# Thirty-two products of a zeroed tile at the head of the tensor engine's program, in a two-layer graph attention kernel

## What is computed

```
scores = q @ k.T * scaling + adj
ctx    = softmax(scores) @ v
x1     = rmsnorm(x + ctx @ wo + bo)
y      = rmsnorm(x1 + silu(x1 @ w1 + b1) @ w2 + b2)     # layer 0, 8 heads, 1536 hidden
x      = layernorm(x + y)
...
x      = layernorm(x + attention(x, adj, adj))          # layer 1, 12 heads, no feed-forward
```

## Time and profile before

| | |
|---|---|
| median of 3 runs | 1896.05 us (1892.42 to 1896.45) |
| the profiled execution, whole | 1891.93 us |
| its span, from the first recorded instruction | 1889.8 us |
| PE busy in it | 1852.5 us, 98% of the span |
| DVE, ACT, POOL busy | 1280.5, 1085.0, 497.7 us |
| mean granted clock of PE | 0.995 |

### The profile page before, as it was taken

One profiled execution on the slowest core, in us unless ns is written; L12 is line 12 of the kernel. 1 busy time (PEld: TensorE's weight loads), 2 busy tenths in 40 slices (PEclk: granted clock), 3 DMA queues, 4 the chain that ended last, 5 costly groups with the idle time before them and its releaser, 6 DMA issues.

```text
span 1889.8 us, 60356 instructions
## 1 busy us (share of the span) xinstructions
PE 1852.5 (98%) x23286; PEld 1820.7 (96%) x23286; DVE 1280.5 (68%) x2507; ACT 1085.0 (57%) x2366; POOL 497.7 (26%) x615
## 2 busy tenths in 40 slices
PE   8999999999999999999999999999999999999997
PEld 7899999999999999999999999999989999999997
DVE  6666666666666666666666666665777877777775
ACT  4555556555556555566555566554556666666665
POOL 0111221211221211221211311212334444444443
PEclk9999999999999999999999999999999999999999
DMA  7644444444444444444444344454233232233322
GB/s 188 186 121 117 119 116 128 116 111 132 117 115 132 112 114 135 113 117 130 111 118 135 110 121 125 111 136 126 57 94 92 84 89 76 87 91 92 92 83 69
DMA packets 268684, 213.46 MB, mean 113 GB/s; under 512 B 142816, under 2 KB 251104, under 8 KB 268640
## 3 DMA queue, kind: packets, MB, share of 16 engines
q1 hardware_dynamic: 268640, 212.85, 41.0%
HBM read 120.33 MB, written 79.69 MB: 106 GB/s over the span
## 4 chain that ended last, share of the span: by engine, by line
PE 88%; SPq 4%; DMA 3%; DVE 2%; ACT 1%; issue 1%; POOL 0%; ACTq 0%; POOLq 0%; DVEq 0%
PE a_banks L477 30%; PE a_bank L477 29%; PE b_bank L1566 15%; PE b_banks L1566 5%; PE b_banks L1618 2%; PE a_banks L550 2%; PE b_banks L1610 2%; PE b_bank L1637 2%; SPq L273 2%; PE a_bank L530 2%; DMA a_work<-ctx_turned 1%; DMA ctx_turned<-a_work 0%; SPq L258 0%; DMA a_work<-x_turned 0%; SPq L264 0%
## 5 line engine op out<-in xcount | busy, mean ns | idle before, releaser
L477 PE MATMUL a_bank<-a_x1t_hi,a_w_hi 128*128 128x256 f32 x1152 | 324.0, 281 | 0.0
L477 PE MATMUL a_bank<-a_x1t_hi,a_w_lo 128*128 128x256 f32 x1152 | 321.3, 279 | 0.0
L477 PE MATMUL a_bank<-a_x1t_lo,a_w_hi 128*128 128x256 f32 x1152 | 321.2, 279 | 0.0
L811 ACT ACTIVATE a_work<-a_bank,a_b 128x256 f32<-128x256 f32 x384 | 160.1, 468 | 196.1 <-PE a_bank L477 195.8
L477 PE MATMUL a_banks<-a_w_hi,a_hid_hi 128*128 128x384 f32 x768 | 258.4, 336 | 1.4 <-DVE a_hid_lo L1031 1.4
L477 PE MATMUL a_banks<-a_w_hi,a_hid_lo 128*128 128x384 f32 x768 | 258.3, 336 | 0.0
L477 PE MATMUL a_banks<-a_w_lo,a_hid_hi 128*128 128x384 f32 x768 | 258.1, 336 | 0.0
L1031 DVE TENSOR_TENSOR a_hid_lo<-a_work,a_hid_hi 128x512 fp32r<-128x512 f32 x192 | 131.9, 699 | 184.7 <-ACT a_hid_hi L816 184.7
L477 PEld LDWEIGHTS a_bank<-a_x1t_hi,a_w_hi 128*128 128x128 f32 x1152 | 217.0, 188 | 2.0
L477 PEld LDWEIGHTS a_bank<-a_x1t_lo,a_w_hi 128*128 128x128 f32 x1152 | 217.8, 189 | 0.0
L477 PEld LDWEIGHTS a_bank<-a_x1t_hi,a_w_lo 128*128 128x128 f32 x1152 | 216.3, 188 | 0.0
(11 more groups left out here) (187 smaller groups left out, 5587.3 us busy)
## 6 DMA issues: line engine op xcount, KB each, us to landing
a_work<-in_x SPq DMA_DIRECT2D x64, 384.0 KB, 3.2
p_turned<-a_work SPq DMA_DIRECT2D x256, 64.0 KB, 2.2
a_work<-p_turned SPq DMA_DIRECT2D x32, 512.0 KB, 3.2
xt_raw<-in_xT SPq DMA_DIRECT2D x32, 384.0 KB, 3.9
ctx_turned<-a_work SPq DMA_DIRECT2D x256, 48.0 KB, 1.7
a_work<-ctx_turned SPq DMA_DIRECT2D x32, 384.0 KB, 3.4
x_turned<-a_work SPq DMA_DIRECT2D x256, 48.0 KB, 1.7
a_work<-x_turned SPq DMA_DIRECT2D x32, 384.0 KB, 3.8
```

Of the source, the lines that this page charges most:

```text
L477: r = pe.matmul(out, lhs[a], rhs[b], start=first and n == 0, stop=last and n == 2)
L811: r = act.activation(silu[:, p % 2, s * GROUP:(s + 1) * GROUP], A[p % 3][:, s * GROUP:(s + 1) * GROUP], ACT.Silu, bias=b1[:, m:m + 1])
```

## The change

DVE zeroes the first of three slices of `x1_t[0]` (128 partitions by 256 elements) before anything else. PE waits for this, and then makes 32 products of that slice with itself, a 128 by 128 stationary part and 256 columns, into `PV_BANK[1]`, ahead of `bias_rows`. Nobody reads them. A new semaphore `zero_set` joins the two.

```
-FILL_FIRST, FILL_X1T, FILL_OUT = 56, 8, (22, 16)
+FILL_BEGIN, FILL_FIRST, FILL_X1T, FILL_OUT = 32, 56, 8, (22, 16)
...
-        ones_set = sem("ones_set")
+        ones_set, zero_set = sem("ones_set"), sem("zero_set")
...
             def begin():
+                pe.wait_ge(zero_set, 1)
+                for _ in range(FILL_BEGIN):
+                    pe.matmul(PV_BANK[1][:, 0:GROUP], x1_t[0][:, 0, 0:P], x1_t[0][:, 0, :], start=True, stop=True,
+                              skip_group_check=True)
                 bias_rows()
                 qk(0)
...
             def begin():
+                dve.memset(x1_t[0][:, 0, :].bitcast(F32), 0.0).then_inc(zero_set, 1)
                 dve.memset(one_row[:], 1.0).then_inc(one_set, 1)
                 split_x(0)
```

## The result

The changed kernel takes 1898.33 us, median of 18 runs, against 1895.03 us for the kernel before on the same chips (18 runs). The ratio is 1.0023, with an interval of 1.0014 to 1.0032: 4.4 us more by the ratio, where I had forecast 0.6 us less (the two medians are 3.3 us apart). The profiled execution of after took 1901.71 us with a span of 1899.9 us; that of before, 1891.93 and 1889.8. The two spans are 10.1 us apart, more than the 4.4 us of the ratio, and part of these 10.1 us will turn out not to belong to the change.

The account below looks back on a forecast made before the run. PE, busy 98% of the span, bounds the kernel; only the start could gain. An earlier clock, limited by the `wq_lo` gate, gives 0.6 us: 1896.05 us median to 1895.5 us, range 1891.2 to 1897.3 us.

Parts of the forecast that it names:

- what bounds the start: From 8.09 us the chain runs through PE's `qk(0)`, `place_bias` and first values, then SP's transfers from 23.31 us.
- the memset: DVE's first instruction, at 0.81 us, estimated at 0.32 us and hidden in 4.3 idle us of DVE.
- the length of the fill: 32 products on PE from 1.3 to 7.25 us, the clock rising at 6.1 us.
- the gate at `wq_lo`: Part 1 of `qk(0)` waits for the low half of `wq`, ending at 11.67 us, and starts at 11.81.
- the last product: The last product of `qk(0)` starts at 16.05 us in place of 16.63, a gain of 0.6 us.
- the 0.5 us that arrive at `swap_v`: SP's first `swap_v` was to come near 22.7 us in place of 23.31, carrying the 0.6 us gain.
- Rival (a): Half clock returns in parts 1 and 2 of `qk(0)`, costing 1.5 us, or zeros leave the clock unchanged: no gain; chance 0.14.
- No transfer is added or moved, none of the queues on SP or POOL changes its order: Behind `qk(0)`, transfers and queues stay as they were, so the 0.6 us passes through `swap_v` unchanged.
- the shift by 0.6 us: From `swap_v` on everything comes 0.6 us earlier; a shift of 0.4 to 0.8 us reaching the end had chance 0.58.
- rival (b): PE's code comes late: the 2.0 us `qk(3)` stall moves into `scores(2)`, leaving 0.7 us more, 1896.8 us; chance 0.14.
- a shift that is gone at the first `ffn1`: Sign of a wrong forecast: the shift at 23 us is lost there, because an unmoved transfer is awaited.
- Rival (c): Later half-clock stretches on PE, 1.5 us each, come or go; two fewer and the 0.6 give 1892 us; chance 0.14.

Follow-up runs that it names:

- restored: The changed kernel with a later fill of 56 products of 256 columns made 24 of 512, 64 instructions fewer; ratio to the kernel before 1.000.
- endpad: The kernel before with 16 small products (64 instructions) in PE's wait ahead of layer 0's last `attn_out`; ratio 1.0014.
- after_again: The changed kernel, unchanged, profiled a second time; 1900.29 us in one run.
- tiny32: The changed kernel with 8 columns in place of 256 in each of the 32 products; ratio to the kernel before 1.0018.
- pad64: The kernel before with 16 small products (64 instructions) at the head, in place of the change's fill; ratio 1.0024.
- fill_pad_b: The changed kernel with 48 small products behind its 32, 256 instructions in all, on a second chip; ratio to the kernel before 0.9995.

## Why the prediction was wrong

**Right.** The reading of what bounds the start, the memset, the length of the fill (1.19 to 7.33 us; worked out 1.3 to 7.25), the gate at `wq_lo`, the last product, and the 0.5 us that arrive at `swap_v`, all of them in the profile of after. Here some luck was in it. The working took the end of the low part of `wq`, 11.67 us, for fixed. Over the 14 profiles it ends between 11.67 and 12.85 us, and with the fill this decides about the gain: the other profiles with the whole fill have `swap_v` at 22.88 to 24.95 us, four of the six later than the 23.31 of before. Rival (a), a half clock within parts 1 and 2, did not come about in after, where the products from 11.80 us on are 0.12 us apart; it did in restored, and cost 1.5 us there, its price in the prediction.

**The step that failed** is the last of the part by part working: "No transfer is added or moved, none of the queues on SP or POOL changes its order", and from `swap_v` on "as a shift". A transfer is moved: the code's own, on a queue that is not SP's or POOL's. In place of the shift by 0.6 us the runs showed 0.23% more, which goes with the place of the code: 64 instructions at the head, of any of three kinds, give 1.0018 to 1.0024, 256 give 0.9991 to 0.9996, and 64 added with 64 taken away give 1.000. The prediction's own last sign of being wrong, a shift that is gone at the first `ffn1`, is there too: 80.41 us in after, 77.91 in before. The prediction did hold the mechanism, in rival (b). It named the code, the 64 instructions, and the earlier trace rows. It failed in three ways there.

- It priced one fetch, that of the stall it saw. Thirty packets of code go through before's queue, and each of them is reached by PE 32 products earlier in the work. The two that showed in after, at the load and in layer 1, are places where before shows no stall at all, so no row of a wait pointed to them.
- At the one that it priced, the opposite happened. The stall did not move into `scores(2)`, it vanished. Code packets start at these counts of PE's recorded instructions: in before 957 (44.3 us), 1470 (63.8 us) and 1498 (68.1 us); in after 1027 (43.9 us), 1197 (56.05 us) and 1529 (67.2 us). The middle packet of after goes while PE is in the large products of `attn_out` and then waits; in before the next one goes only at 1470, when 270 more instructions are through, on which PE spends under 4 us, as they belong to the small products. The code that was late in before is in time in after, and what it meets now is the load. The "against" of (b) ("such a refill may be asked for earlier too") was right, and its conclusion "nothing is lost" overlooked where the packet would go then. Why the packet is let go at 1197 in the one and only at 1470 in the other, the runs don't settle.
- Its price was 0.7 us at a chance of 0.14. Measured is 4.4 us by the ratio (2.7 to 6.1 us). What can be put to a place is layer 1's: a second stall of 1.5 to 1.8 us in `pv`, a stretch around it that takes 3.1 us more (mean of after's two profiles less that of before's three), and 2.7 us by endpad's ratio (0.6 to 4.7). Where the rest arises stays open. After and after_again are 2.0 us later than before's mean at 174 us, but tiny32 and pad64, which lose as much in the end, are not.

The Trainium skill (Runtime: NRT & Kernel Launch, Instruction fetch mechanics) says that code comes in blocks of 256 instructions, fetched ahead, and that crossing from one to the next is mostly hidden. The first half agrees: the stalls found lie 256 or 512 counts apart, and 256 added instructions are neutral where 64 are not. The second half is where I leant on it too much. It holds for most of the 30 packets, and not where 96 products are through in 1.22 us, nor for the load, which a packet held up by some 4 us: 64 instructions cost 0.23%. The measurement decides.

**Rival (c)** and the range. I took the scatter of the runs for half-clock stretches that come and go. The clock column did change a little (0.90 for 0.93 at 50 to 100 us), but the larger part is the length of the loop's turn, 40.41 or 40.63 us, that is 5.9 us over 27 turns with the clock at 1.00 in both. Of all 14 profiles, 5 have the short turn (40.41 to 40.43 us), and 9 the long. Among the eight kernels whose loop has its old place, it is 4 and 4; among the six others, 1 and 5. That is too few to say that the place sets the odds; if it did, a part of the ratio would come from it. It is hardly the whole: of the 18 runs each, the fastest of after is 5.4 us above the fastest of before and the slowest 5.7 us above the slowest, where other odds alone would leave both ends. (Against that, pad64's fastest run, 1890.34 us, is no slower than before's fastest on its chip, 1890.83.) What decides the turn stays open. The range, up to 1897.3 us, was drawn around the runs of before and had room for 0.7 us of (b) only; 1898.33 us lies above it.

## What to carry to other kernels

Instructions that are added ahead of a tuned program can cost more than their time: they shift all later code against the points where blocks of it are fetched. Before pricing a change at the head, look for all code packets in the trace, and for two kinds of neighbours at the new distance: runs of small products, which use up a block in a few us, and large transfers that the path waits for (the second kind was held up here, but that it cost time at the end is not shown). To tell such a cost from the change's own effect, run the old kernel with as many neutral instructions, and the new one filled up to a whole block (here 256), or with as many instructions taken away elsewhere; if the loss goes, it is the place. And profile a kernel more than once before a microsecond at its head is called gained: the two profiles of after differ by 0.7 us at 23 us.

## What the hardware showed that I had not expected

- In the stalls on code of over 1 us, all but one, PE went on 2.3 to 2.9 us after the start of a code packet. In before's layer 1 the instructions at hand lasted 2.9 us, and there was no stall.
- A code packet of 0.02 MB and 1.4 us can go with a delay of 4 us of a 512 KB load (7.8 us for 3.5), because the load is over only when its last sixteenth is.
- A stall on code of 2.0 to 3.4 us can be free or nearly so (in `qk(3)`: 3.3 us in fill_pad_b, at a ratio of 0.9995) while one of 1.5 us in layer 1 comes with a kernel that is 2.7 us slower (endpad, interval 0.6 to 4.7 us). Losing the free one gained nothing.
- 32 products of 8 columns with 128-column weights take 6.99 us, 0.22 us each: no less than the 0.213 us of 256 columns at half clock. Fewer columns did not shorten the fill.
- Equal products at a granted clock of 1.00 follow each other 114 or 118 ns apart, by the execution: half of those in each turn of the loop, for the whole loop.
